# Column totals of the attention loop as two rounded passes, with the maxima's spread ahead of the total

## The reference, cut to what matters

```
scores = einsum('bsghd,btgd->bghst', q, k) * scale
p = softmax(scores, axis=-1)
out = einsum('bghst,btgd->bsghd', p, v)
```

## Time and profile before

| what | us |
|---|---|
| median of 3 runs | 427.75 |
| lowest, highest | 425.83, 428.95 |
| the profiled execution's own time | 427.4 |
| its span, from first to last instruction | 425.6 |

### The profile page before, as it was taken

The page is one execution under the profiler, slowest core; times in us unless marked ns, Lnnn a source line. Parts: engine busy times, 40 slices in busy tenths (PEclk is TensorE's granted clock), DMA queues, the critical chain, the costliest instruction groups (busy, mean ns, idle before and its releaser), DMA issues.

```text
span 425.6 us, 6868 instructions
## 1 busy us (share of the span) xinstructions
PE 414.7 (97%) x2427; PEld 292.2 (69%) x2433; DVE 347.2 (82%) x699; ACT 248.8 (58%) x780; POOL 35.8 (8%) x58
## 2 busy tenths in 40 slices
PE   8999999999999999999999999999999999999897
PEld 3453455788885767778676686785486799837596
DVE  5889999987999899689899998978887787746831
ACT  2478898688547777748986677664505263220220
POOL 0010000040000001100001000010010004101000
PEclk9999999999999999999999999999999999999999
DMA  7599120500002015993554835688337979730000
GB/s 240 226 191 415 39 85 2 199 2 26 27 2 99 1 51 123 201 306 78 132 124 92 198 70 108 155 187 359 74 78 246 390 267 241 151 125 2 2 2 25
DMA packets 14591, 56.80 MB, mean 133 GB/s; under 512 B 1824, under 2 KB 2912, under 8 KB 13280
## 3 DMA queue, kind: packets, MB, share of 16 engines
q1 hardware_dynamic: 11104, 39.31, 25.3%
q0 software_dynamic: 3456, 17.11, 21.4%
HBM read 41.40 MB, written 0.26 MB: 98 GB/s over the span
## 4 chain that ended last, share of the span: by engine, by line
PE 74%; DVE 12%; issue 6%; DMA 4%; ACT 3%; POOL 1%; SPq 0%; DVEq 0%; ACTq 0%; POOLq 0%
PE PS L482 11%; PE PS L1817 10%; PE PS L453 8%; PE PS L454 8%; PE PS L455 8%; PE PS L1846 3%; PE PS L535 3%; PE PS L1287 3%; DMA lutw_dt.float<-luttmp_dt.float 2%; PE PS L1832 2%; DMA raw_dt.float<-in_wk_nat 1%; PE PS L492 1%; PE PS L1153 1%; PE PS L1135 1%; PE PS L1295 1%
## 5 line engine op out<-in xcount | busy, mean ns | idle before, releaser
L605 ACT ACTIVATE sq_dt.float<-PS 128x128 bf16<-128x128 f32 x256 | 67.0, 279 | 27.0 <-PE PS L455 20.5
L482 PE MATMUL PS<-s_dt.float,ctx_ring_dt.float 128*128 128x512 f32 x128 | 57.8, 593 | 0.0
L605 ACT ACTIVATION_READ_ACCUMULATOR sq_dt.float<-PS 128x1 f32 x256 | 53.6, 210 | 0.0
L453 PE MATMUL PS<-wkc_dt.float32r,ctx_hi_dt.float32r 128*128 128x512 f32 x128 | 51.5, 402 | 0.1
L454 PE MATMUL PS<-wkT_dt.float32r,ctx_hi_dt.float32r 128*128 128x512 f32 x128 | 50.0, 390 | 0.0
L455 PE MATMUL PS<-wkc_dt.float32r,ctxT_ring_dt.float32r 128*128 128x512 f32 x128 | 49.9, 390 | 0.0
L687 ACT ACTIVATE luttmp_dt.float<-low_bit_dt.float,vec_dt.float,small_dt.float 128x1536 f32<-128x1536 uint8 x24 | 38.5, 1654 | 8.5 <-DMA lutw_dt.float<-luttmp_dt.float 8.5
L1817 PE MATMUL PS<-wch_dt.float,xs_dt.float 128*128 128x512 f32 x96 | 42.0, 592 | 0.0
L482 PEld LDWEIGHTS PS<-s_dt.float,ctx_ring_dt.float 128*128 128x128 f32 x128 | 23.6, 190 | 23.6 <-issue 23.0
L700 POOL DMA_DIRECT2D lutw_dt.float<-luttmp_dt.float x21 | 18.2, 869 | 234.7 <-DVE luttmp_dt.float L694 234.7
L694 DVE SCALAR_TENSOR_TENSOR luttmp_dt.float<-idx_dt.float,luttmp_dt.float 128x1536 f32<-128x1536 uint8 x21 | 36.6, 1753 | 0.0
(11 more groups left out here) (304 smaller groups left out, 851.3 us busy)
## 6 DMA issues: line engine op xcount, KB each, us to landing
lutw_dt.float<-luttmp_dt.float POOLq DMA_DIRECT2D x21, 768.0 KB, 6.1
wch_dt.float<-in_chunks SPq DMA_DIRECT2D x5, 1024.0 KB, 7.9
ctxT_ring_dt.float<-in_ctxT SPq DMA_DIRECT2D x8, 512.0 KB, 3.4
ctx_ring_dt.float<-in_ctx SPq DMA_DIRECT2D x8, 512.0 KB, 3.9
keysT_dt.float<-in_ctxT SPq DMA_DIRECT2D x8, 512.0 KB, 7.0
keys_dt.float<-in_ctx SPq DMA_DIRECT2D x8, 512.0 KB, 8.0
zu_dt.float<-in_wproj SPq DMA_DIRECT2D x1, 2048.0 KB, 7.2
A_first_dt.float<-in_wproj SPq DMA_DIRECT2D x1, 2048.0 KB, 10.2
```

Of the source, the lines that this page charges most:

```text
L453: nc.tensor.matmul(o, x_hi, hi[:, c, :], start=c == 0, stop=False)
L482: last = nc.tensor.matmul(mix_bank(b, c), keysr[k][:, t, c * 128:c * 128 + 128], sS[k][:, t, :], start=t == 0, stop=t == KT - 1)
L605: last = nc.scalar.activation(sq[:, (4 * hf + g) * D:(4 * hf + g + 1) * D], key_bank(b, 2 * t + hf)[:, g * D:(g + 1) * D], ACT.Square, acc ...
```

## The change

For batches 0 to 5 `total` is made from two rounded parts of ps2. ACT copies ps2 to ps_hi (fp32r, new `hi_of_sum`, between its second and third leaf), DVE subtracts to get ps_lo (new `lo_of_sum`, between `maxima` and `shift`), and PE adds two matmuls of one record each with a rounded matrix of ones, ones_r, which POOL makes once, ahead of its copies at L709. On PE `spread(b)` now stands ahead of `total(b-1)`. On DVE `sums(b-1)` stands ahead of `lo_of_A(b+1)` for b > 1, and `term(b-1, 0)` behind `normalise(b-1)`. Totals of batches 6 and 7 stay as they were.

```diff
@@ -68,6 +68,7 @@
     ("s", 2 * KT * NK, LOOP, LAST, "wch"), ("catx", NH * T, LOOP, LAST, "zu"),
     ("px", CT * NH * 64, LOOP, LAST, "catc"), ("qtmp", 1280, LOOP, LAST, "catc"),
     ("vecs", 5 * NK, LOOP, LAST, "raw"), ("ctx_hi1", CT * NK, LOOP, LAST, "raw"),
+    ("ps_lo", NK, LOOP, LAST, "catc"), ("ps_hi", NK, LOOP, LAST, "raw"),
     ("keys", B * KT * C, TAIL, LATE, "catc"),
     ("lutw", NLUT, LOOP, LATE, "xs"), ("luttmp", 3 * CT * IPAD, LOOP, LATE),
     ("idx", NLUT // 4, FRONT, LATE), ("low_bit", NLUT // 4, FRONT, LATE),
@@ -78,6 +79,7 @@
     ("hT_hi", CT * T, TAIL, TAIL), ("hT_lo", CT * T, TAIL, TAIL),
     ("ffn", 2 * IT * T, LATE, LATE), ("rot", 2 * 512 + 2 * 2 * 128 + 2 * 256 + 2 * C, LATE, LATE),
     ("rotact", 4 * 1024, LATE, LATE), ("probs", 2 * TT * NK, LATE, LATE),
+    ("ones_r", 128, FRONT, LAST),
 ]
 
 
@@ -135,7 +137,7 @@
 
         tensors = {(name, fp32): tensor(name, fp32) for name in size}
         for name in ("zu", "catc", "lutw", "wkc", "wkT", "ctx_hi0", "ctx_hi1", "ctxT_ring", "A_hi", "A", "catx", "A_first", "beta", "gu_a", "gu_b", "gu_hi", "hT_hi",
-                     "hT_lo"):
+                     "hT_lo", "ps_hi", "ps_lo", "ones_r"):
             tensors[name, fp32r] = tensor(name, fp32r)
         PS = ctx.enter_context(nc.psum_tensor("PS", [128, 4096], fp32))
 
@@ -239,6 +241,7 @@
                                                                                    "krs_ready", "beta_turned"))
         st_full, scaled, sum_read, mxf_ready, tr_full, m_ready, mb_full = (sem(n) for n in (
             "st_full", "scaled", "sum_read", "mxf_ready", "tr_full", "m_ready", "mb_full"))
+        ps_hi_ready, ps_split, ones_ready = sem("ps_hi_ready"), sem("ps_split"), sem("ones_ready")
         shifted, p_ready, psum_ready, sum_full, r_ready, pctx, px_ready = (sem(n) for n in (
             "shifted", "p_ready", "psum_ready", "sum_full", "r_ready", "pctx", "px_ready"))
         v_full, v_read, catx_ready, proj_out = (sem(n) for n in ("v_full", "v_read", "catx_ready", "proj_out"))
@@ -334,6 +337,7 @@
         sq = buf("sq", 1024, dtype=bf16)
         mx, nm, R = buf("vecs", 512), buf("vecs", 512, skip=512), buf("vecs", 512, skip=1024)
         ps2 = buf("vecs", 2, 512, skip=1536)
+        ps_hi, ps_lo, ones_r = (buf(name, n, dtype=fp32r) for name, n in (("ps_hi", 512), ("ps_lo", 512), ("ones_r", 128)))
         px = buf("px", CT, NH, 64)
         catx = buf("catx", NH, T, dtype=fp32r)
         idx = buf("idx", 3, CT * IPAD, dtype=u8)
@@ -384,8 +388,8 @@
                 maxima(b)
                 if prev and more:
                     mix(b - 1, 1 - k, 1)
+                    spread(b)
                     total(b - 1)
-                    spread(b)
                 elif prev:
                     mix(b - 1, 1 - k, 1, range(2))
                     spread(b)
@@ -487,8 +491,16 @@
             def total(b):
 
 
-                pe.wait_ge(psum_ready, b + 1)
+                split = not (isinstance(b, int) and b >= 6)
+                if split:
+                    pe.wait_ge(ps_split, b + 1)
+                else:
+                    pe.wait_ge(psum_ready, b + 1)
                 pe.wait_ge(scaled, 4 * KT * 2 - 1 if isinstance(b, int) and b == B - 1 else 4 * b + 7)
+                if split:
+                    nc.tensor.matmul(bank(2), ones_r, ps_hi, start=True, stop=False)
+                    nc.tensor.matmul(bank(2), ones_r, ps_lo, start=False, stop=True).then_inc(sum_full, 1)
+                    return
                 nc.tensor.matmul(bank(2), ones, ps2[:, 0, :], start=True, stop=True).then_inc(sum_full, 1)
 
             def project_core(parts):
@@ -560,6 +572,7 @@
             keys(1, 1, range(3, KT))
             project_core((2,))
             pe.wait_ge(ld_wvT, 16)
+            pe.wait_ge(ones_ready, 1)
             scores(1, 1, range(2))
             project_core((3,))
             scores(1, 1, range(2, KT))
@@ -621,8 +634,12 @@
                 if more:
                     split_A(act, b + 1)
                 if b:
-                    for m in range(3):
-                        leaf(act, b - 1, m)
+                    leaf(act, b - 1, 0)
+                    leaf(act, b - 1, 1)
+                if prev and more:
+                    hi_of_sum(b - 1)
+                if b:
+                    leaf(act, b - 1, 2)
                 if prev and more:
                     inverse(b - 1)
                 if next_context:
@@ -638,6 +655,10 @@
             def exponentials(b, k):
                 act.wait_ge(shifted, b + 1)
                 nc.scalar.activation(sS[k], sS[k], ACT.Exp, scale=SCALE).then_inc(p_ready, 1)
+
+            def hi_of_sum(b):
+                act.wait_ge(psum_ready, b + 1)
+                nc.scalar.activation(ps_hi, ps2[:, 0, :], ACT.Copy).then_inc(ps_hi_ready, 1)
 
             def inverse(b):
 
@@ -703,6 +724,8 @@
             pool.wait_ge(proj_full, 6)
             for m in range(3):
                 pool.dma_start(idx[:, m, :], io["idx"][:, m, :]).then_inc(ld_idx[m], 16)
+            pool.wait_ge(ld_const, 16)
+            nc.gpsimd.tensor_copy(ones_r, ones).then_inc(ones_ready, 1)
             pool.wait_ge(ld_wpc, 16)
             pool.wait_ge(low_full, 1)
             for i in range(4):
@@ -761,15 +784,16 @@
                     even_part(2)
                     lo_of_context(dve, 2, 0)
                     dve.wait_ge(bits_ready, 3)
+                sums(b - 1, 1 - k)
                 if b > 1:
                     lo_of_A(dve, b + 1)
-                sums(b - 1, 1 - k)
                 maxima(b)
                 if b == 1:
                     lo_of_A(dve, 2)
-                term(dve, b - 1, 0)
+                lo_of_sum(b - 1)
                 shift(b, k)
                 normalise(b - 1, 1 - k)
+                term(dve, b - 1, 0)
                 if pair is not None:
                     read_values(pair, 0)
                     quantize_values(pair, 0)
@@ -839,6 +863,10 @@
                     dve.wait_ge(sum_full, b)
                 self_step(nc.vector.tensor_tensor(ps2, sS[k][:, 0:2, :], sS[k][:, 2:4, :], ALU.add))
                 nc.vector.tensor_tensor(ps2[:, 0, :], ps2[:, 0, :], ps2[:, 1, :], ALU.add).then_inc(psum_ready, 1)
+
+            def lo_of_sum(b):
+                dve.wait_ge(ps_hi_ready, b + 1)
+                nc.vector.tensor_tensor(ps_lo, ps2[:, 0, :], ps_hi, ALU.subtract).then_inc(ps_split, 1)
 
             def maxima(b):
 
```

## The result

The changed kernel takes 429.42 us (median of 10, 428.51 to 432.15) beside 427.25 for the kernel before (10 runs, 425.83 to 428.95) on the same chip: ratio 1.0061, interval 1.0037 to 1.0085. It is slower by 0.4 to 0.9%. Its profiled execution took 428.92 us with a span of 426.8, against 427.4 and 425.6.

What follows compares the result with a forecast made beforehand. PE's matmul queue was taken to set the pace in the loop. Step 1's +2.2 us less 0.8 us saved gave +1.4 us: 428.8 profiled, 429.2 us forecast as median, range 425.3 to 432.0.

Steps and rivals of the forecast that it cites:

- The pair of products: PE's total: two rounded products cost 0.46 us instead of 0.86, saving 0.40 us per changed total, 2.4 us at most.
- Rival D: Changed totals: a rounded pair costs the old total's 0.86 us, no savings; +3.4 us, 431.2; chance 0.07.
- Step 1: PE waits for VectorE's new subtraction, so ScalarE's inverse and all behind it come later: +2.2 us, bounds +1.0 to +2.6.
- Steps 2 to 6: Each total saves 0.40 us, but late VectorE spends the savings of steps 2, 3 and 4 at step 4's end.
- score tile of batch 4: End of step 3: VectorE scales it 1.9 us late, ready at 206.55 when PE wants it at 206.56, just in time.
- rival C: Steps 3 to 6: VectorE closes the loop, each step 0.69 us longer; +4.6 us, 432.4; chance 0.11.
- Rival B: Whole loop: the saving arrives whole, six times 0.40, -2.4 us, 425.4; chance 0.27.
- rival E: PE's new stalls: granted clock falls, step 1's 48 key products at half speed cost 11 us more, about 440; chance 0.03.
- A: Whole kernel: the forecast itself, +0.5 to +2.5 us, 428.2 to 430.4; chance 0.52.

Runs made afterwards that it cites:

- f1: Changed kernel with step 1 as before and two of the four split_weights parts moved out of step 4; 425.24 us, ratio 0.9943.
- e1: Changed kernel with step 1 made as before, totals 1 to 5 in parts; 427.68 us, ratio 1.0003.
- e2: Changed kernel with lo_of_sum(0) ahead of lo_of_A(2) in step 1; 428.12 us, one run.
- f2: Changed kernel with only its moves of order: every total the fp32 product of before, no copy or subtraction; 429.36 us, ratio 1.0047.
- e3: Changed kernel with two of the four split_weights parts moved from step 4 into steps 6 and 7; 427.16 us, ratio 0.9992.
- g4: Changed kernel again, unchanged, for a second profile; 429.67 us, ratio 1.0049.
- f3: Changed kernel with only the rounded parts, the order of total, sums and term as before; 429.48 us, ratio 1.0050.
- g3: f1 once more, the same kernel; 424.62 us, ratio 0.9928.
- g2: Changed kernel with e3's weights, and in step 1 VectorE's sums and low part ahead of lo_of_context and lo_of_A(2); 424.79 us, ratio 0.9925.
- g1: f3 with eight bf16 products of 512 columns on PE in step 1's wait, results unread; 429.05 us, ratio 1.0045.

## Why the prediction was right, and where it was not

**The pair of products** was sized right: 0.32 us from the first to the second, 0.23 behind it, and 0.40 us for each total (step 2 took 1.66 - 1.23 = 0.43 us less, by the starts of the queries' high part, L588 and now L601; f1's five steps agree). Only the forecast of 0.81 us or so from the transposes to the keys left the start-up out: it is 0.35 + 0.32 + 0.23 = 0.90, as measured. That changes no saving, because the start-up is paid once in either kernel. Rival D is refuted.

**Step 1, +2.2 us**: right in each link. On before's clock, that is with the 0.52 us added, the subtraction began at 136.23 (forecast 136.24), PE started at 136.97 (136.98), the inverse at 137.75 (137.78), and PE waits 0.99 us for the squares where 0.54 stood. e1 took all of it away (-2.18 against the changed kernel, by loops), e2 half. What the prediction didn't see is that the exchange on PE alone would have cost half as much: with the subtraction out of the way step 1 is still 1.0 us longer than before (e2), and 1.16 without any subtraction (f2). The two don't add, because PE goes by the one that comes last.

**Steps 2 to 6.** Lateness of PE from the loop's start, forecast in brackets: after step 1 +2.2 (2.2), after step 2 +1.75 (1.8), after step 3 +1.4 (1.4), after step 4 +2.2 (2.2), after step 5 +1.9 (1.8), at the spread of step 7 +1.44 (1.4). Where VectorE is late by itself, after steps 3 and 5, this is taken from the next spread, which stands one total (0.86 us) earlier in PE's queue: 0.54 + 0.86 = 1.4, and 1.02 + 0.86 = 1.9. The score tile of batch 4 was just in time as said (PE's loader waits 0.19 us). In step 4 the maxima were done at 213.91 + 0.16 = 214.07 and PE began the spread at 214.71: a margin of 0.6 us, forecast 0.5, behind which rival C would have begun. It did not.

**Rival B** fell by both of its own counter-arguments: step 1 runs over ScalarE, step 4 over VectorE. f1 shows that the saving arrives once both are taken away: 2.0 us for the five totals that it changes. The other 0.8 us of its loop are before's own stall.

**What was sized wrong.** First, the stalls in the expectations of e3 and f1: the idle figure was taken as the price, but 1.76 is 2.0 and 0.54 is 0.8. (f2's expectation came out, 172.12 for 172.1, because it used the difference of two stalls.) The forecast was spared, because it worked with the times at which the score tile was ready and not with idle time. Second, rival E. It was given 0.03 and 11 us, by the assumption that the clock would stay low for all 48 products of step 1. It was back at 1.00 by 142 us, so the fall costs 0.8 us in g4 and 1.3 us in f3. It also seems to come much more often: in the changed kernel 8 of 20 executions (3 of the first ten, 5 of g4's) have a mean granted clock of 0.995 or 0.996, as g4's profile has, and these took 429.77 to 432.54 us. The others have medians of 428.92 and 428.66, which is 1.7 and 1.2 us above the medians of before beside them; the loop of the first profile says 1.44.

The median rose by 2.2 us where 1.4 was forecast. That the forecast of 429.2 lies only 0.2 below the measured 429.42 is luck: it started from 427.75, and before's median of ten is 427.25, so a start 0.5 too high nearly made up for a rise 0.8 too small. The agreement of the mechanism is that of the first profile's loop, at full clock (+1.44); g4's loop is +2.22. That the remaining 0.8 us of the median is the clock fits, but isn't shown for the executions without a trace: before too has 0.996 in 3 of 23 and 3 of 22, e3 has it in 4 of 12, and in e1 and f1, which have no new wait in step 1, the profile shows a fall in the tail. For f1, in a stretch where the changed kernel kept 1.00:

```profile
395.00:400.00 5.00, 3.96 (x72) 2.66 (x73) 3.06 (x8) 1.19 (x5) 0.00 (x0) 0.70 0.01 3
```

Its tail took 131.73 us for 130.54 in g3, the same kernel. Which of the two places it was in each execution stays open.

Two slips of the sum change nothing: the upper end of A is 427.75 + 2.5 = 430.25 and not 430.4, and the score tile of batch 4 was forecast 205.8 - 203.83 = 2.0 us late where 1.9 is written (measured 1.85).

## What to carry to other kernels

A saving on the bounding engine arrives only in stages in which no other engine's result is the last to come; find those stages before counting the saving, and take the second engine's slack there (here four weight parts and one term on VectorE) as part of the change. Where an operand gets a new producer on a late engine, the stage with the longest chain behind it needs to be left as it was, or its engine's order changed so that the producer comes first. Both gave -0.6 to -0.75% with two weight parts moved (f1, g3 and g2), where all six totals as changed gave +0.6%. Some 0.8 of the 2.8 us by which the loops of f1 and g2 are shorter than before come from the moved weights and not from the totals. Read what a stall costs from the times of the products around it, not from its idle figure.

## What the runs showed of the hardware

A wait of PE of 2.3 us (f3), or two of 0.6 and 1.1 us around four transposes (g4), was followed by a granted clock of 0.50, with rounded products of 512 columns 0.43 us apart instead of 0.23; by 142 us it was back at 1.00. The same kernel with the same waits kept 1.00 in another profile, so such waits make the fall possible and not certain. With eight bf16 products inside the wait (g1) the clock stayed at 1.00 in the one profile that was taken, and in 9 of 10 executions the mean was 1.00; of f3's four executions without them two were at 0.996. That the products prevent the fall is likely by these numbers and not certain.

The Trainium skill ("TensorE: Matmul & The Clock Gate", "What's actually happening") says that the array's default is the throttled state and that activity, not frequency settings, releases it. The windows of f3 and g1 agree: from 138 to 140 us, 0.50 without the added products and 1.00 with them.
